# Fused cross-attention and low-bit feed-forward kernel: mask added inside PSUM, exponent read from PSUM, wider column blocks for the attention product, and other places for weight pieces, rows, keys and moves

## The chip, the cores and the metric

One core of one Trainium2 chip. The metric is the device time of one launch in microseconds. TensorE is called PE here (its weight loads PEld), VectorE DVE, ScalarE ACT, GpSimd POOL and SyncE SP.

## What is computed

```python
q = rope((layernorm(x) @ wq) per head)      # 32 query heads of 128
k = rope((ctx @ wk) per head); v = ctx @ wv # 8 key/value heads, each for 4 query heads
scores = q @ k.T / sqrt(128) + mask         # batch 8, 256 rows, 256 keys
x = x + (softmax(scores) @ v) @ wo
w = lut4[o, 4-bit code(qweight)]            # 1024 x 1024
x = x + layernorm(x) @ w.T + bias
```

All is fp32. The norm of every row of the second layer norm is far below the threshold of 64, so the reference's 8-bit branch is never taken and the kernel computes the 4-bit one alone. Each fp32 product is made of three passes over a rounded part (HI) and a rest (LO) of both operands (`PASSES`).

## The kernel before, in words

**Stages.** Batches of keys and values and the decoding of the 4-bit weights come first (to about 394 us), then the attention, then the feed-forward product (from about 2246 us). The change lies in the attention.

**Units, rounds, halves.** The attention runs over `NU` = 256 units. A unit is one query head of one batch entry: 256 rows by 256 keys, scores as two tiles of 128 x 256 in PSUM bank 0 (`s_ps`). Four units in a row (`REP`) share keys and values; 16 units (`UNITS`, 4 batch entries) form a round, which has its own four `wq` and four `wo` pieces; 8 rounds form a half of the batch. Below, "step 4" means a unit whose number leaves 4 when divided by 16.

**PE's order in a step** (L868 to L879): the 6 score matmuls of this unit (`scores`, L800, 256 columns), 12 matmuls of a query projection for a later unit (`query`, L784), in two steps of some rounds four transposes of a normalized row (`turn_side`, L811), 12 matmuls of the output projection of the unit three back (`project`, L862), and in even steps the 6 attention matmuls of the two units before (`attend(u - 2)`, L834, 512 columns: two units at once).

**From scores to transposed probabilities.** DVE adds the mask and takes the row maximum in one instruction per tile (`add_mask`, L1652, result to `probs` in SBUF, the score columns read with a stride of four by `by_blocks`), then negates the maximum (L1659). ACT takes the exponent in place in SBUF (`exponent`, L1177). DVE inverts the sum (`invert`, L1664), POOL scales (`normalize`, L1809), DVE transposes 32 x 32 blocks (`turn_blocks`, L1668), and four DMAs of 64 KB issued by SP spread the blocks over the partitions (`move_blocks`, L590). ACT rounds the result (`turned_high`, L1190), DVE computes the rest (`turned_low`, L1673), and then `attend` may start. ACT's `turned_high` and DVE's `turned_low` of an odd unit stand, in the two engines' orders, behind the exponent and the inversion of the even unit after it. For the units in `PE_TURNS` (1, 253, 254, 255) PE transposes instead (L823) and nothing is moved.

**Weight pieces.** A piece is 512 KB, loaded into the single buffer `raw` (`load_weights`, L395, waits for the rest of the piece before it), rounded by ACT (L1228) and split by DVE (`weights_split`, L1379). `PIECE` puts the pieces of a round at steps 0, 1, 3, 4 (`wo`) and 8, 9, 12, 13 (`wq` of the next round); ACT's and DVE's parts stand at the end of that step. In rounds 1 to 7 one row tile of the next half is layer-normalized on the side: `ROW_AT` (step 0; DVE's `row_var` there, `row_scale` at the end of step 1), `SIDE` (steps 5 and 6, transposed halves split and stored through `raw`).

**SP's order** (L594 to L642) is one queue: values (L461), keys (`load_keys`, L454, waits for the scores of this unit), mask (L448), pieces, moves, rows. Keys for the next four units are loaded at steps that leave 3 when divided by 4, behind the moves of the unit before. The moves of a unit also wait until the attention product two units back has been made (`o_mm`).

**Other DVE work of a step** (L1697 to L1750): `query_cos`, `query_add`, `query_low` (rotary embedding of a projected query, in odd steps), `output_low` (L1678), `add_projection` (four adds of 512 columns, L1694, every fourth step).

**Columns of the attention product.** `pT_keys` gives L834 its 512 moving columns as 16 runs of 32.

```python
pT_keys = R[:, 4608:6656].rearrange("p (l q k j) -> p l k q j", l=2, k=TS, j=QUAD)
def by_blocks(row): return row.rearrange("p (m b) -> p b m", b=P // QUAD)
pe.wait_ge(s_read, u + 1)      # scores(u): the mask of unit u - 1 has read bank 0
```

## Time and profile before

| | us |
|---|---|
| median of 3 runs | 2436.77 (2436.72 to 2442.36) |
| profiled execution | 2438.7 |
| its span | 2436.9 |
| PE busy | 2376.7 (98%) |
| PEld busy | 1999.4 |
| DVE busy | 1658.1 (68%) |
| ACT busy | 1150.0 (47%) |
| POOL busy | 501.6 (21%) |
| mean granted PE clock | 0.997 |

The profiled execution took 2438.7 us, 1.8 us more than its span (what lies around the first and last instruction). Matmuls are pipelined and their ends modelled, so "busy" of PE holds short waits too; the distance from the start of one group of matmuls to the start of the next is the better measure.

### The profile page before, as it was taken

What the parts mean: (1) busy time and instruction counts of PE and PEld (TensorE: products, weight loads), DVE (VectorE), ACT (ScalarE), POOL (GpSimd) and SP (SyncE); (2) the same over time, 40 slices, a digit from 0 to 9 for tenths busy, and PEclk for the clock granted to TensorE, in tenths of its full rate; (3) what the DMA queues carried; (4) which work ended last, traced back from release to release, by engine and by line L of the source; (5) the groups of instructions that cost most, each with busy time, mean ns of one, the idle gap of its engine ahead of it and who ended that gap; (6) DMA issues with size and microseconds to landing.
All of it is one profiled execution on the core that took longest, in us unless ns stands there. A gap on an engine that the chain in (4) does not pass through costs nothing.

```text
span 2436.9 us, 35037 instructions
## 1 busy us (share of the span) xinstructions
PE 2376.7 (98%) x11982; PEld 1999.4 (82%) x11982; DVE 1658.1 (68%) x3810; ACT 1150.0 (47%) x2475; POOL 501.6 (21%) x674
## 2 busy tenths in 40 slices
PE   9999999999999999999999999999999999999999
PEld 8999997878787878787878788778888887887887
DVE  8887776666666666666666666666666666675553
ACT  5555434454645455555544444444444444443110
POOL 1000001222222222222222222222222222222111
PEclk9999999999999999999999999999999999999999
DMA  6466567534343444434357633333333333335211
GB/s 257 159 215 194 183 220 230 158 111 117 108 126 104 113 114 116 114 111 118 106 162 233 196 103 95 99 102 111 96 108 104 96 98 106 103 93 186 87 70 52
DMA packets 323185, 321.44 MB, mean 132 GB/s; under 512 B 31680, under 2 KB 259264, under 8 KB 323008
## 3 DMA queue, kind: packets, MB, share of 16 engines
q1 hardware_dynamic: 323008, 319.20, 43.5%
q8 instruction: 96, 1.57, 0.3%
q14 instruction: 81, 0.66, 0.1%
HBM read 181.73 MB, written 71.30 MB: 104 GB/s over the span
## 4 chain that ended last, share of the span: by engine, by line
PE 75%; DMA 6%; DVE 6%; SPq 4%; ACT 4%; issue 4%; POOL 2%; ACTq 0%; DVEq 0%
PE bank L784 20%; PE bank L862 19%; PE bank L746 7%; PE bank L900 7%; PE bank L723 7%; PE bank L834 7%; PE bank L800 5%; SPq L590 3%; DMA raw<-in_L_xattn_wo 3%; ACT probs L1177 1%; DVE probs L1652 1%; DMA raw<-in_L_xattn_wq 1%; POOL probs L1809 1%; DVE residual L1694 1%; ACT weights_split L1228 1%
## 5 line engine op out<-in xcount | busy, mean ns | idle before, releaser
L784 PE MATMUL bank<-acts_split,weights_split 128*128 128x512 f32 (+1 forms) x3168 | 751.4, 386 | 3.0 <-DVE rope_a L1617 0.4
L862 PE MATMUL bank<-weights_split,small_split 128*128 128x512 f32 x3072 | 741.8, 390 | 4.0 <-DVE small_split L1678 3.7
L862 PEld LDWEIGHTS bank<-weights_split,small_split 128*128 128x128 f32 x3072 | 573.9, 188 | 125.9 <-DVE small_split L1678 7.9
L784 PEld LDWEIGHTS bank<-acts_split,weights_split 128*128 128x128 f32 x3168 | 568.1, 189 | 113.9 <-issue 6.1
L1809 POOL TENSOR_SCALAR probs<-probs,row_numbers 128x256 f32<-128x256 f32 x512 | 289.3, 577 | 1343.6 <-DVE row_numbers L1664 1343.6
L1177 ACT ACTIVATE probs<-probs,row_numbers 128x256 f32<-128x256 f32 x512 | 256.5, 502 | 385.0 <-DVE row_numbers L1659 384.9
L1668 DVE STREAM_TRANSPOSE probs<-probs 128x512 f32<-128x512 f32 x252 | 179.2, 711 | 174.7 <-POOL probs L1809 174.7
L1801 POOL TENSOR_TENSOR rope_x<-rope_x,sin_t 128x512 f32<-128x512 f32 (+1 forms) x132 | 167.1, 1266 | 403.0 <-ACT rope_x L1159 398.0
L834 PE MATMUL bank<-small_split 128*128 128x512 f32 x762 | 208.6, 410 | 41.9 <-DVE small_split L1673 28.7
L800 PEld LDWEIGHTS bank<-small_split 128*128 128x128 f32 x1536 | 219.1, 191 | 33.4 <-DMA small_split<-k_scratch 10.8
L800 PE MATMUL bank<-small_split 128*128 128x256 f32 x1536 | 227.7, 285 | 5.3 <-DMA small_split<-k_scratch 4.6
L1673 DVE TENSOR_TENSOR small_split<-small_split 128x512 fp32r<-128x512 f32 x252 | 179.8, 714 | 61.9 <-ACT small_split L1190 61.9
L834 PEld LDWEIGHTS bank<-small_split 128*128 128x128 f32 x762 | 139.5, 190 | 92.5 <-DVE small_split L1673 38.1
L1652 DVE CUSTOM_DVE_ANT_0 probs<-bank,mask_tile 128x256 f32<-128x256 f32 x512 | 196.6, 421 | 26.3 <-PE bank L800 25.3
L1228 ACT ACTIVATE weights_split<-raw 128x1024 fp32r<-128x1024 f32 x120 | 127.3, 1061 | 161.7 <-DMA raw<-in_L_xattn_wq 81.8
L1379 DVE TENSOR_TENSOR weights_split<-raw,weights_split 128x1024 fp32r<-128x1024 f32 x120 | 146.7, 1223 | 73.2 <-ACT weights_split L1228 72.6
L746 PE MATMUL bank<-small_split,weights_split 128*128 128x256 f32 x1536 | 187.6, 284 | 1.0 <-DVE weights_split L1372 0.6
L746 PEld LDWEIGHTS bank<-small_split,weights_split 128*128 128x128 f32 x1536 | 185.4, 192 | 2.1 <-issue 1.0
L900 PE MATMUL bank<-weights_split,acts_split 128*128 128x512 f32 x768 | 178.5, 391 | 0.0
L723 PE MATMUL bank<-acts_split,small_split 128*128 128x512 f32 x768 | 178.1, 391 | 0.1
L1194 ACT ACTIVATE small_split<-bank 128x512 fp32r<-128x512 f32 x127 | 75.7, 596 | 207.3 <-PE bank L834 207.2
L1664 DVE RECIPROCAL row_numbers<-row_numbers 128x2 f32<-128x2 f32 x256 | 42.4, 166 | 190.4 <-ACT probs L1177 190.4
(120 smaller groups left out, 2284.0 us busy)
## 6 DMA issues: line engine op xcount, KB each, us to landing
small_split<-probs SPq DMA_DIRECT2D x1008, 64.0 KB, 2.1
raw<-in_L_xattn_wq SPq DMA_DIRECT2D x61, 512.0 KB, 3.7
raw<-in_L_xattn_wo SPq DMA_DIRECT2D x60, 512.0 KB, 3.7
k_scratch<-small_split SPq DMA_DIRECT2D x64, 256.0 KB, 2.3
v_scratch<-small_split SPq DMA_DIRECT2D x32, 512.0 KB, 2.9
x_scratch<-raw SPq DMA_DIRECT2D x64, 256.0 KB, 2.8
acts_split<-x_scratch SPq DMA_DIRECT2D x32, 512.0 KB, 5.8
mask_tile<-in_mask_BxSxS_ff SPq DMA_DIRECT2D x64, 256.0 KB, 3.0
```

Of the source, the lines that this page charges most:

```text
L723: done = pe.matmul(wide_ps[t][:, :], ctxT[:, c, a, t * P:(t + 1) * P], wv_s[:, c, m, n * BANK:(n + 1) * BANK], start=c == 0 and k == 0, st ...
L746: done = pe.matmul(k_ps[g % 2], wk_s[:, c, a, g * DK:(g + 1) * DK], ctxT[:, c, m, :], start=c == 0 and i == 0, stop=c == C - 1 and i == 2)
L784: last = pe.matmul(query_bank(j)[:, 0:wide], wq_s[:, h, c, a, :], xT[:, c, m, b * S:b * S + wide], start=c == 0 and i == 0, stop=c == C - ...
L800: last = pe.matmul(s_ps[:, t * S:(t + 1) * S], q_s[:, Q_SLOT[u], a, t * P:(t + 1) * P], k_s[:, m, :], start=i == 0, stop=i == 2)
L834: last = pe.matmul(o_ps[:, :], v_s[:, k, a, :], pT_keys[:, m, k], start=k == 0 and i == 0, stop=k == TS - 1 and i == 2)
L862: last = pe.matmul(out_ps[part][:, :], o_s[:, a, u % 2 * S + t * P:u % 2 * S + (t + 1) * P], wo_s[:, h, m, n * BANK:(n + 1) * BANK], start ...
L900: last = pe.matmul(out_ps[f % 2 * NN + n][:, :], xT[:, c, a, f % HT * P:(f % HT + 1) * P], w4_s[:, c, m, n * BANK:(n + 1) * BANK], start=c ...
L1177: last = act.activation(row, row, ACT.Exp, bias=neg_max[:, u % 2, t:t + 1], accum_out=row_sum[:, u % 2, t:t + 1])
L1652: last = dve.tensor_tensor_reduce(out=by_blocks(probs[:, u % 2, t, :]) if u in PE_TURNS else prob_part(u, t), in0=by_blocks(s_ps[:, t * S: ...
L1668: dve.transpose(prob_rows[:, u % 2, :], prob_rows[:, u % 2, :]).then_inc(p_blocks, 1)
L1673: dve.tensor_tensor(pT_s[:, LO, u % 2, :], source, pT_s[:, HI, u % 2, :].bitcast(F32), ALU.subtract).then_inc(pT_lo, 1)
L1809: done = pool.tensor_scalar(row, row, row_inv[:, u % 2, t:t + 1], 1.0, ALU.mult, ALU.mult)
```

## The change

The score bank is now the place where mask and scores are added (L1652 writes to bank 0, contiguous; the mask is no longer permuted on the host); the exponent reads bank 0 with the stride of four and writes `probs`. So bank 0 is free for the next scores only after the exponent (`exp_done`), and the wait until a `probs` slot has been moved away goes from DVE to ACT. A row of `probs` is laid out so that `pT_keys` has 8 runs of 64 columns. Pieces go to steps 0, 2, 4, 5 and 6, 8, 10, 12; DVE's splits, but for steps 4 and 5, go to the step after, between `invert` and `turn_blocks`. Row tiles go to step 8, their stored halves to steps 13 and 14. In SP's queue most pieces are issued ahead of an odd unit's moves, and of the moves of the unit before a key load two are issued ahead of the keys and two behind, the mask behind them. Units 247 and 251 are turned by PE too. In the first steps some operations of queries and early `wo` pieces trade places.

```diff
-    PE_TURNS = (1, NU - 3, NU - 2, NU - 1)
+    PE_TURNS = (1, NU - 9, NU - 5, NU - 3, NU - 2, NU - 1)
-            PIECE[g * UNITS + (0, 1, 3, 4)[h]] = ("wo", g, h)
+            PIECE[g * UNITS + (0, 2, 4, 5)[h]] = ("wo", g, h)
-            PIECE[g * UNITS + (8, 9, 12, 13)[h]] = ("wq", g + 1, h)
+            PIECE[g * UNITS + (6, 8, 10, 12)[h]] = ("wq", g + 1, h)
+    SAME_STEP = (4, 5)
+    LOAD_LAST = (6, 8)
-    ROW_ROUND = {e: e - A_ROWS + 1 for e in range(A_ROWS, NT)}
-    SIDE = {UNITS * g + 5 + j: (e, j) for e, g in ROW_ROUND.items() for j in range(2)}
-    ROW_AT = {UNITS * g: e for e, g in ROW_ROUND.items()}
+    ROW_AT = {UNITS * (e - A_ROWS) + 8: e for e in range(A_ROWS, NT)}
+    SIDE = {u + 5 + j: (e, j) for u, e in ROW_AT.items() for j in range(2)}
-        pT_keys = R[:, 4608:6656].rearrange("p (l q k j) -> p l k q j", l=2, k=TS, j=QUAD)
+        pT_keys = R[:, 4608:6656].rearrange("p (l a k n) -> p l k a n", l=2, k=TS, n=TS * QUAD)
-        prob_parts = prob_t[:, :].rearrange("p (s b t m) -> p s t b m", s=2, b=P // QUAD, t=TS)
+        prob_parts = prob_t[:, :].rearrange("p (s b k t i) -> p s t b k i", s=2, b=P // QUAD, k=TS, t=TS)
...
-                if u % REP == REP - 1 and u + 1 < NU:
-                    load_keys(u + 1)
-                    load_mask(u + 1)
-                if u % REP == REP - 1 and u in PIECE:
-                    load_weights(u)
+                if u % REP == REP - 1:
+                    if u + 1 < NU:
+                        load_keys(u + 1)
+                    if u - 1 not in PE_TURNS:
+                        move_blocks(u - 1, (2, 3))
+                    if u + 1 < NU:
+                        load_mask(u + 1)
+                if u + 1 in PIECE and (u + 1) % UNITS not in LOAD_LAST:
+                    if u - 1 in SIDE:
+                        sp.wait_ge(x_stored, 4 * 16 * (SIDE[u - 1][0] + 1))
+                    load_weights(u + 1)
...
                 if u % 2 == 0 and u not in PE_TURNS:
-                    move_blocks(u)
-                if u % REP != REP - 2 and u + 1 in PIECE:
+                    move_blocks(u, (0, 1) if u % REP == REP - 2 else range(P // QUAD))
+                if u + 1 in PIECE and (u + 1) % UNITS in LOAD_LAST:
...
-                pe.wait_ge(s_read, u + 1)
+                pe.wait_ge(exp_done, u)
...
             def exponent(u):
+                if u - 2 in PE_TURNS:
+                    act.wait_ge(pT_tr, PE_TURNS.index(u - 2) + 1)
+                elif u >= 2:
+                    act.wait_ge(pT_in[u % 2], 4 * 16 * landed(u - 2))
                 act.wait_ge(s_max, u + 1)
                 for t in range(TS):
-                    row = prob_part(u, t)
-                    last = act.activation(row, row, ACT.Exp,
+                    row, scored = probs[:, u % 2, t, :], s_ps[:, t * S:(t + 1) * S]
+                    if u not in PE_TURNS:
+                        row = prob_parts[:, u % 2, t]
+                        scored = scored.rearrange("p (k i b) -> p b k i", k=TS, i=QUAD)
+                    last = act.activation(row, scored, ACT.Exp,
...
             def add_mask(u):
-                if u - 2 in PE_TURNS:
-                    dve.wait_ge(pT_tr, PE_TURNS.index(u - 2) + 1)
-                elif u >= 2:
-                    dve.wait_ge(pT_in[u % 2], 4 * 16 * landed(u - 2))
                 dve.wait_ge(s_mm, 1 + u + 1)
                 for t in range(TS):
                     last = dve.tensor_tensor_reduce(
-                        out=by_blocks(probs[:, u % 2, t, :]) if u in PE_TURNS else prob_part(u, t),
-                        in0=by_blocks(s_ps[:, t * S:(t + 1) * S]),
-                        in1=mask_t[:, t, :].rearrange("p (b m) -> p b m", b=P // QUAD), scale=1.0, scalar=-3.0e38, op0=ALU.add, op1=ALU.max,
+                        out=s_ps[:, t * S:(t + 1) * S], in0=s_ps[:, t * S:(t + 1) * S],
+                        in1=mask_t[:, t, :], scale=1.0, scalar=-3.0e38, op0=ALU.add, op1=ALU.max,
...
                 invert(u)
                 if u == 0:
                     output_weights_lo(2)
-                if u == 1:
-                    output_weights_lo(3)
+                if u - 1 in PIECE and (u - 1) % UNITS not in SAME_STEP:
+                    split_piece(u - 1)
                 if u % 2 == 0 and u and u - 1 not in PE_TURNS:
                     turned_low(u - 1)
                 if u not in PE_TURNS:
                     turn_blocks(u)
+                if u == 2:
+                    output_weights_lo(3)
...
-                if u in PIECE:
-                    kind, _, h = PIECE[u]
-                    weights_split(A_PIECES + PIECE_AT[u], kind, h)
+                if u in PIECE and u % UNITS in SAME_STEP:
+                    split_piece(u)
```

## Rows read from the trace of the kernel before

**Rows 1.** The page, part 1: busy time and share of the engines.
```profile
PE 2376.7 (98%) x11982; PEld 1999.4 (82%) x11982; DVE 1658.1 (68%) x3810; ACT 1150.0 (47%) x2475; POOL 501.6 (21%) x674
```

**Rows 2.** The chain that ended last: four PE groups (start, time until the next link).
```profile
1029.03 2.75 PE bank L784 x12
1031.78 2.72 PE bank L862 x12
1034.50 0.71 PE bank L800 x6
...
1040.68 1.42 PE bank L834 x6
```

**Rows 3.** Groups of instructions, shapes apart: the attention matmuls, with PE's idle before.
```profile
L834 PE MATMUL bank<-small_split 128*128 128x512 f32 x762 | 208.6, 410 | 41.9 <-DVE small_split L1673 28.7 <-issue 13.1
```

**Rows 4.** Single lines of L800, L834, L862: ns min/median/max, first and last start.
```profile
L800 PE MATMUL bank<-small_split x1536: 274/283/416, 394.2 to 2231.1; 128*128 128x256 f32 x192
...
  DMA small_split<-k_scratch: 15.5, 25
...
L834 PE MATMUL bank<-small_split x762: 397/401/766, 414.2 to 2230.2; 128*128 128x512 f32 x191
...
L862 PE MATMUL bank<-weights_split,small_split x3072: 387/389/504, 422.0 to 2245.6; 128*128 128x512 f32 x192
```

**Rows 5.** Timeline, units 65 to 68 (start, us; in brackets idle before and releaser).
```profile
871.41 0.71 DVE L1668 STREAM_TRANSPOSE probs<-probs 128x512 f32<-128x512 f32 x1 [1.06 <-POOL probs L1809]
...
872.28 0.88 PE L800 MATMUL bank<-small_split 128*128 128x256 f32 x6
...
874.07 1.22 DVE L1379 TENSOR_TENSOR weights_split<-raw,weights_split 128x1024 fp32r<-128x1024 f32 x1
...
876.01 0.42 DVE L1652 CUSTOM_DVE_ANT_0 probs<-bank,mask_tile 128x256 f32<-128x256 f32 x1
...
879.53 1.66 PE L834 MATMUL bank<-small_split 128*128 128x512 f32 x6 [0.91 <-issue]
...
887.22 0.87 PE L800 MATMUL bank<-small_split 128*128 128x256 f32 x6
...
889.75 1.06 ACT L1228 ACTIVATE weights_split<-raw 128x1024 fp32r<-128x1024 f32 x1 [2.36 <-DMA raw<-in_L_xattn_wo]
...
890.85 1.23 DVE L1379 TENSOR_TENSOR weights_split<-raw,weights_split 128x1024 fp32r<-128x1024 f32 x1 [1.34 <-ACT weights_split L1228]
...
891.99 0.42 DVE L1652 CUSTOM_DVE_ANT_0 probs<-bank,mask_tile 128x256 f32<-128x256 f32 x1
...
895.46 1.69 PE L834 MATMUL bank<-small_split 128*128 128x512 f32 x6 [1.57 <-DVE small_split L1673]
```

**Rows 6.** Timeline, units 0 to 2: the first attention product.
```profile
409.24 1.23 DVE L1393 TENSOR_TENSOR weights_split<-residual,weights_split 128x1024 fp32r<-128x1024 f32 x1 [2.89 <-ACT weights_split L919]
...
414.24 2.90 PE L834 MATMUL bank<-small_split 128*128 128x512 f32 x6 [3.39 <-issue]
```

**Rows 7.** One stretch: length, busy us per engine, then granted clock, DMA share, GB/s.
```profile
408.00:426.00 18.00, 14.61 (x58) 11.87 (x58) 10.69 (x24) 8.41 (x19) 4.84 (x6) 0.81 0.21 55
```

**Rows 8.** Groups, shapes apart: operations near to the changed ones on DVE and ACT.
```profile
L1177 ACT ACTIVATE probs<-probs,row_numbers 128x256 f32<-128x256 f32 x512 | 256.5, 502 | 385.0 <-DVE row_numbers L1659 384.9
...
L1652 DVE CUSTOM_DVE_ANT_0 probs<-bank,mask_tile 128x256 f32<-128x256 f32 x512 | 196.6, 421 | 26.3 <-PE bank L800 25.3
...
L1190 ACT ACTIVATE small_split<-small_split 128x512 fp32r<-128x512 f32 x252 | 158.2, 628 | 21.3 <-DMA small_split<-probs 16.0
...
L1194 ACT ACTIVATE small_split<-bank 128x512 fp32r<-128x512 f32 x127 | 75.7, 596 | 207.3 <-PE bank L834 207.2
...
L1270 DVE TENSOR_TENSOR rope_a<-bank,cos_t 128x256 f32<-128x256 f32 x32 | 13.6, 424 | 20.7 <-ACT rope_x L932 20.2
```

**Rows 9.** DMA issues: KB each and median us from issue to landing.
```profile
small_split<-probs SPq DMA_DIRECT2D x1008, 64.0 KB, 2.1
raw<-in_L_xattn_wq SPq DMA_DIRECT2D x61, 512.0 KB, 3.7
```

More of the change, by code:

```diff
@@ L253, in build_xattn_ffn @@
         pT_ps = bank[2]
-        pT_cols = bank[2][:, :].rearrange("p (a t k j) -> p t k a j", t=TS, k=TS, j=QUAD)
+        pT_cols = bank[2][:, :].rearrange("p (a k t j) -> p t k a j", t=TS, k=TS, j=QUAD)
         o_ps = bank[5]
@@ L327, in prob_part @@
         def prob_part(u, t):
-            return probs[:, u % 2, t, :] if u in PE_TURNS else prob_parts[:, u % 2, t]
+            if u in PE_TURNS:
+                return probs[:, u % 2, t, :]
+            return prob_parts[:, u % 2, t].rearrange("p b k i -> p (b k) i")
         def fold(view, units):
@@ L582, in _, with move_blocks @@
             sp.wait_ge(v_stored, 16 + 16 * (NB * len(V_TURNS) - 3))
-            def move_blocks(u):
+            def move_blocks(u, places=range(P // QUAD)):
                 sp.wait_ge(p_blocks, blocks(u))
                 sp.wait_ge(o_mm, 1 + u // 2)
-                for a in range(P // QUAD):
+                for a in places:
                     done = sp.dma_start(pT_moved[:, LO, u % 2, a, :].bitcast(F32),
@@ L844, in attend_one @@
                     for i, (a, m) in enumerate(PASSES):
-                        last = pe.matmul(o_ps[:, half_of], v_s[:, k, a, :], pT_keys[:, m, k, u % 2 * (S // QUAD):(u % 2 + 1) * (S // QUAD)],
+                        last = pe.matmul(o_ps[:, half_of], v_s[:, k, a, :], pT_keys[:, m, k, u % 2 * (P // QUAD):(u % 2 + 1) * (P // QUAD)],
                                          start=k == 0 and i == 0, stop=k == TS - 1 and i == 2)
@@ L1699, in _ @@
                     query_cos(DONE[u - 1])
-                if u >= LAG and u % REP == REP - 1:
+                output_first = u % REP == REP - 1 or u > NU - 14
+                if u >= LAG and u % 2 and output_first:
                     output_low(u - LAG)
@@ L1703, in _ @@
                     add_mask(u)
-                if u >= LAG and u % REP == 1:
+                if u >= LAG and u % 2 and not output_first:
                     output_low(u - LAG)
+                if u == 2:
+                    turned_low(0)
+                if u - 1 in PE_TURNS:
+                    turned_low(u - 1)
                 if u == AHEAD:
@@ L1709, in _ @@
                     query_add(DONE[u - 1])
-                if u - 1 in PE_TURNS:
-                    turned_low(u - 1)
                 if u - 1 in DONE:
@@ L1730, in _ @@
                     query_add(DONE[u])
-                if u % 2 and u - 1 not in PE_TURNS:
+                if u % 2 and u > 1 and u - 1 not in PE_TURNS:
                     turned_low(u - 1)
```

32 lines of the change are left out of this document (15 added, 17 removed).

## The prediction

> **What bounds the kernel now.** The page first: PE is busy 2376.7 of 2436.9 us, DVE 68%, ACT 47% [rows 1]. So PE's order of work sets the time, and only two things can shorten it: cheaper matmuls, or fewer waits between them. The chain of waits gives the undisturbed pace: 0.71 us for the scores, 2.75 for a query projection, 2.72 for an output projection, 1.42 for an attention product [rows 2]. An odd step is the first three, 6.18 us; an even one has the fourth too, 7.60. A round of 16 is 110.2. The scores run from 394.2 to 2231 us [rows 4], 1837 us for 255 steps. Sixteen rounds are 1763; less the last step, narrower or missing queries at the end and missing projections at the start (about 23), plus double queries in the first two steps and the 56 transposes of rows (about 12), that leaves about 1750. So some 87 us are lost in the attention, 5 a round: the most that better order can bring.
>
> Where they are lost, by the groups and single lines: PE sat idle 41.9 us before L834 and at most 15.5 us before the scores for keys [rows 3, 4]. The rest are waits of 0.1 to 0.4 us, which the modelled ends of matmuls cover up, and slow clock after long ones.
>
> Why `attend` waits shows in the timeline [rows 5]. In step 2 (scores at 872.28) it could start 6.18 later, at 878.46, and starts at 879.53: 1.07 late. In step 4 (scores at 887.22) it is due at 893.40 and starts at 895.46: 2.06 late. In both, the mask instruction of that even unit stands 3.5 us ahead of it (876.01 to 879.53, 891.99 to 895.46): mask, exponent, then `turned_high` and `turned_low` of the odd unit, which stand behind them in ACT's and DVE's orders. So the rule for an even step: if its mask starts later than 6.18 - 3.5 = 2.7 us after its scores, PE waits for the difference. Here it was 3.7 and 4.8 us late. What made it late is DVE: in step 1 a piece's split at 874.07 and after it the scale of the row tile, in step 3 a split that waited for ACT, which waited 2.36 us for the piece's DMA. Steps 2 like this one are 8 (about 1.1 us each), steps 4 are 15 (about 1.8 on average, 1.3 to 2.9).
>
> **The change, part by part.** All against the profiled execution's 2438.7 us, which is 1.9 above the median of 2436.77; the saving is carried over to the median.
>
> *Splits into DVE's gap.* In an odd step DVE idles 1.06 us for POOL between `invert` and `turn_blocks` (the first line of [rows 5]). A split is 1.22. Six of eight splits go there, so each costs 0.16 us of DVE's order instead of 1.22, and a split after step 3's mask no longer waits for a DMA issued in the same step. With that, step 4's mask should start at 4.8 - 1.22 - 1.3 (the wait) + 0.16, about 2.4 us: no wait of PE, barely. Of 15 x 1.8 = 27 us I take 24, keeping a fifth of a us a round for moves that land late. In step 2 the row's scale leaves too: 3.7 - 1.06 - 0.72 = 1.9 us. I take 8 of 8 x 1.1 = 9 us.
>
> *Rows to steps 8, 13 and 14.* The scale (0.72 us from the end of the split, 875.29, to the mask [rows 5]) now burdens step 10, in seven rounds, which loses its split of step 9 in exchange. Nothing; at worst 7 x 0.5 = 3.5.
>
> *Splits of steps 4 and 5 stay at the step's end.* Step 6's mask gets 1.22 us in front; by the pattern of steps 10 and 14 before, which had the same split in front and hardly waited, it comes to about 2.6, just under 2.7. I take 3 us lost; 0 to 15 x 1 = 15 are the ends.
>
> *Start.* `attend(0)` came 3.39 us late, behind a split that waited 2.89 for ACT [rows 6], and the clock granted over the 18 us around it was 0.81 [rows 7], which is 0.19 x 18 = 3.4 us more at the lower of the two levels. The early `wo` piece 3 moves behind it. I take 5 of 6.8.
>
> *Keys.* They are issued behind two moves instead of four, and no longer behind a late `turn_blocks`, so about 1.2 us earlier. The 15.5 us counts PEld's waits; the ones seen were up to 1 us. I take 8; 4 to 12.
>
> *Wider runs.* L834 takes 1.42 / 6 = 237 ns a matmul, L862 with the same 512 columns in one run 2.72 / 12 = 227 [rows 2]; their shortest rows differ by the same 10 ns [rows 4]. If it is the 16 runs, 8 runs give back half: 762 x 5 ns = 4 us. Ends: 0 (it is something else) and 7.6.
>
> *Mask in PSUM, exponent from PSUM.* The mask instruction writes to PSUM, which no DVE row shows; it reads the bank with a stride of four now at 421 ns, and a DVE instruction of the same size that reads a bank contiguously takes 424 [rows 8]. I take 421 after; ends 380 and 480. ACT reads PSUM faster than SBUF, 596 against 628 ns for 512 columns [rows 8], so the exponent (502) could lose 30 ns; but with a stride of four, which no ACT row shows. I take 480 and 1100 (below) as ends, 490 as value, by DVE's row. Worth nothing on PE: the exponents' gain of 0.02 us a unit ends in slack.
>
> *The new wait.* Scores of unit u wait for the exponent of u - 1 instead of its mask. What is queued behind is all of PE. The mask of unit 66 starts 3.7 us after its scores [rows 5]; from there two masks and two exponents take 2 x 421 + 2 x 502 ns [rows 8], with the small ones between some 2.1 us: 5.8, where the next scores come after 7.6 at the earliest. In an odd step a mask even 2.4 us late gives 4.5 of 6.18. Slack 1.7, so nothing; an exponent pair 1.7 us longer would hold PE up in odd steps. The wait for moved `probs`, now on ACT, is for moves issued a step earlier: they land 2.1 us after issue [rows 9], over 3 us ahead.
>
> *Two more units turned by PE.* Eight transposes of 128 columns, under 0.5 us a unit, for eight DMAs fewer and two steps near the end without their landing. Nothing; -3 to +1.
>
> *SP.* A piece's issue before an odd unit's moves is one more issue of 0.6 us, but DVE's split, for which it waits, ends as `turn_blocks` (0.71 us) begins, so it is out before the moves may go. Nothing; the landing is a rival.
>
> *Small waits after splits in the gap* (query_cos 0.16 later, PE's next query waits for it in some steps): 3 us lost.
>
> Sum: 24 + 8 + 5 + 8 + 4 - 3 - 3 = 43 us. 2438.7 - 43 = 2395.7 for a profiled execution, **2394** for the median.
>
> **A rule that speaks against it.** DVE's row says that a stride of four in PSUM costs nothing. The Trainium skill (Advanced Engine Details and Errata, PSUM Cachelines) says that PSUM has lines of 8 bytes and that every two consecutive elements should be contiguous for best throughput; the trace disagrees for DVE and has nothing for ACT. By the skill the exponent would be slower; by the row not.
>
> **The rivals.**
>
> *The exponent is slow with the stride (slower, 8%).* L1190 takes 628 ns for 512 columns, at most 1.23 ns each; a read at half pace adds up to 0.31 us to an exponent, at a quarter 0.93, twice per unit. At 0.62 us a unit the 2.7 us of the rule become 2.1: step 6 waits 0.5, steps 4 and 8 (2.4) 0.3, and the queries behind `query_cos` about 0.5 in four steps: 3 us x 16 = 48, time 2442. At 1.86 a unit all eight even steps wait, 0.9 on average above the half-pace case: 2500 or more. It decides from an exponent of about 800 ns. For it: only the missing row. Against: DVE's.
>
> *Moves behind pieces land late (18%).* Five odd units a round (steps 15, 1, 3, 9, 11) now send their moves right behind 512 KB that take 3.7 us, where a move takes 2.1 [rows 9]. Up to 1.6 later. The worst placed moves (turned 0.3 after the next scores, four issues, landing near 4.3) have 0.4 us of slack against 6.18 - 1.5. At 0.8 later PE loses 0.4 x 5 x 16 = 32: 2426; at 1.6, 96: 2490. Against: the fourth move leaves 2.4 us after the piece, and most units will be turned earlier. 14% for 2412 to 2435, 4% for above.
>
> *The wait moves to step 6 (14%).* Piece 5 is loaded only when piece 4 is split; if it lands late, DVE waits as step 3 did, and 15 x 1.9 = 28 us come back: 2422.
>
> *Nothing happens* (the waits have another cause): within the chance of no change.
>
> **How the numbers follow.** 60% for the forecast, own range 2378 (all ends good) to 2412. Over 0.3%, 7 us, is what a measurement tells: faster below 2429.5, slower above 2444. Faster: 60 + 14 + 9 = 83%; same 7% ; slower 10% (most of the exponent's 8, and 3 of late moves). The range 2378 to 2430 leaves out some 6% below and 15% above.
>
> **What would show it.** L834 idle from 41.9 to under 12 us; L834 groups 1.39 to 1.40 instead of 1.42; mask of step 4 starting about 2.4 us after the scores, of step 2 about 1.9; L1177 at 480 to 500 ns; L800 idle for keys near nothing; DVE's wait for POOL down from 1.06 to nothing in steps with a split; the clock never at 0.81 near 414 us. Wrong: L1177 above 700; L1190 waiting for DMA over 30 us in all (16.0 now, rows 8); L834 waits gathered in step 6.

## The result, and the profile after

| | before | after |
|---|---|---|
| median, us | 2438.90 (4 runs) | 2419.68 (4 runs, 2417.57 to 2420.95) |
| ratio, 95% interval | | 0.9919, 0.9902 to 0.9936 |
| profiled execution, us | 2438.7 | 2419.55 |
| its span, us | 2436.9 | 2417.8 |
| mean granted PE clock | 0.997 | 0.999 |

The change is faster by 19 us (the medians' difference; the before's median here has one run more than the one shown above). 43 were forecast. From the first scores to the last, the attention took 1836.3 us before and 1815.3 after: 21 us, so the whole difference lies there (the rest of the program took 2 us longer).

The page after, part 1 (busy time) and the groups of part 5 (busy, mean ns of one | PE's or the engine's idle before it, and what ended it):

```profile
PE 2360.4 (98%) x11990; PEld 2001.1 (83%) x11990; DVE 1665.4 (69%) x3808; ACT 1132.6 (47%) x2475; POOL 573.7 (24%) x674
...
L791 PE MATMUL bank<-acts_split,weights_split 128*128 128x512 f32 (+1 forms) x3168 | 753.2, 387 | 40.5 <-DVE rope_a L1633 40.4
...
L1824 POOL TENSOR_SCALAR probs<-probs,row_numbers 128x256 f32<-128x256 f32 x512 | 365.5, 726 | 1276.0 <-DVE row_numbers L1675 1276.0
L1193 ACT ACTIVATE probs<-bank,row_numbers 128x256 f32<-128x256 f32 x512 | 238.2, 470 | 373.8 <-DVE row_numbers L1670 373.7
L1664 DVE CUSTOM_DVE_ANT_0 bank<-bank,mask_tile 128x256 f32<-128x256 f32 x512 | 206.6, 445 | 109.3 <-PE bank L807 109.3
...
L807 PE MATMUL bank<-small_split 128*128 128x256 f32 x1536 | 224.0, 282 | 1.7 <-ACT probs L1193 1.7
L841 PE MATMUL bank<-small_split 128*128 128x512 f32 x762 | 196.3, 393 | 4.6 <-issue 2.7
...
L1206 ACT ACTIVATE small_split<-small_split 128x512 fp32r<-128x512 f32 x250 | 158.1, 632 | 35.4 <-DMA small_split<-probs 26.0
```

Beside [rows 1, 3, 8]: `attend` (now L841) waits 4.6 us where it waited 41.9. That is the wait that the change was forecast to remove, and it is gone. But the query projection (now L791) waits 40.5 us, for `query_cos` on DVE (L1633). And POOL is busy 573.7 us instead of 501.6 [rows 1], with the same 674 instructions: its scaling of a row tile (now L1824) takes 726 ns. The two groups in the kernel before:

```profile
L784 PE MATMUL bank<-acts_split,weights_split 128*128 128x512 f32 (+1 forms) x3168 | 751.4, 386 | 3.0 <-DVE rope_a L1617 0.4
...
L1809 POOL TENSOR_SCALAR probs<-probs,row_numbers 128x256 f32<-128x256 f32 x512 | 289.3, 577 | 1343.6 <-DVE row_numbers L1664 1343.6
```

3.0 us of waiting and 577 ns. In the changed kernel, the waits of PE grouped by waiter and releaser, over the attention (us in all, times, longest):

```profile
PE bank L791 <- DVE rope_a L1633: 40.4, 55, 1.8
PE bank L869 <- DVE small_split L1689: 3.4, 7, 0.9
PE bank L841 <- issue: 2.7, 5, 1.4
```

How the new wait comes about, in the timeline of an odd step, unit 71 (start, duration, engine, line; in brackets idle before and releaser):

```profile
915.97 0.17 DVE L1675 RECIPROCAL row_numbers<-row_numbers 128x2 f32<-128x2 f32 x1 [1.15 <-ACT probs L1193]
...
916.05 1.20 DVE L1395 TENSOR_TENSOR weights_split<-raw,weights_split 128x1024 fp32r<-128x1024 f32 x1
...
916.23 1.83 POOL L1824 TENSOR_SCALAR probs<-probs,row_numbers 128x256 f32<-128x256 f32 x2 [6.10 <-DVE row_numbers L1675]
...
918.09 0.71 DVE L1679 STREAM_TRANSPOSE probs<-probs 128x512 f32<-128x512 f32 x1 [0.83 <-POOL probs L1824]
...
918.73 0.65 DVE L1633 SCALAR_TENSOR_TENSOR rope_a<-bank,cos_t 128x512 f32<-128x512 f32 x1
...
919.44 3.02 PE L791 MATMUL bank<-acts_split,weights_split 128*128 128x512 f32 x12 [1.00 <-DVE rope_a L1633]
```

The split (L1395) stands where DVE used to wait for POOL. POOL's pair of row tiles, started beside it, takes 1.83 us; in the kernel before it took, in two steps after each other (odd, then even):

```profile
870.45 0.93 POOL L1809 TENSOR_SCALAR probs<-probs,row_numbers 128x256 f32<-128x256 f32 x2 [6.24 <-DVE row_numbers L1664]
...
878.41 1.36 POOL L1809 TENSOR_SCALAR probs<-probs,row_numbers 128x256 f32<-128x256 f32 x2 [5.66 <-DVE row_numbers L1664]
```

0.93 us with DVE idle, 1.36 with `turned_low` beside it. These are no chance picks: in the changed kernel's trace the pair takes 1.82 to 1.83 us beside each of 90 splits, and in the kernel before 0.93 in the 136 cases without a longer DVE instruction beside it and 1.36 (median) in the 116 with `turned_low`. In the changed kernel `turn_blocks` (L1679) thus still waits 0.83 us for POOL, as DVE waited 1.06 before [rows 5]: the split filled DVE's gap, and the gap was made longer by it. `query_cos` behind it comes late, and PE waits 1.00 us. The theory from here on: **a split in the gap slows the very POOL instruction that the gap waits for.** The rivals: the forecast's 0.16 us for each split is right and PE waits for something that comes later in DVE's order; or DVE is merely busy for too long.

### The profile page after: what moved, and what is told of

Its sections match the earlier page's. It is cut to its first block, busy times and chain, and to the rows that moved or that the text cites. A ratio compares the mean times of both kernels' runs of the same rounds, so it can differ in the third digit from the quotient of the medians.

```text
span 2417.8 us, 35170 instructions
## 1 busy us (share of the span) xinstructions
PE 2360.4 (98%) x11990; PEld 2001.1 (83%) x11990; DVE 1665.4 (69%) x3808; ACT 1132.6 (47%) x2475; POOL 573.7 (24%) x674
## 4 chain that ended last, share of the span: by engine, by line
PE 55%; DVE 20%; POOL 9%; ACT 7%; issue 4%; DMA 3%; SPq 2%; ACTq 0%; DVEq 0%
PE bank L791 14%; PE bank L869 12%; POOL probs L1824 8%; PE bank L907 7%; PE bank L753 7%; PE bank L730 6%; ACT probs L1193 5%; DVE residual L1705 5%; PE bank L841 4%; DVE bank L1664 3%; PE bank L807 3%; DVE probs L1679 2%; DMA small_split<-probs 2%; DVE rope_a L1633 2%; SPq L593 1%
## 5 line engine op out<-in xcount | busy, mean ns | idle before, releaser
L791 PE MATMUL bank<-acts_split,weights_split 128*128 128x512 f32 (+1 forms) x3168 | 753.2, 387 | 40.5 <-DVE rope_a L1633 40.4
L869 PE MATMUL bank<-weights_split,small_split 128*128 128x512 f32 x3072 | 741.3, 390 | 3.5 <-DVE small_split L1689 3.4
L791 PEld LDWEIGHTS bank<-acts_split,weights_split 128*128 128x128 f32 x3168 | 567.3, 189 | 155.2 <-DVE rope_a L1633 29.0
L869 PEld LDWEIGHTS bank<-weights_split,small_split 128*128 128x128 f32 x3072 | 574.4, 188 | 124.1 <-DVE small_split L1689 5.3
L1824 POOL TENSOR_SCALAR probs<-probs,row_numbers 128x256 f32<-128x256 f32 x512 | 365.5, 726 | 1276.0 <-DVE row_numbers L1675 1276.0
L1193 ACT ACTIVATE probs<-bank,row_numbers 128x256 f32<-128x256 f32 x512 | 238.2, 470 | 373.8 <-DVE row_numbers L1670 373.7
L1664 DVE CUSTOM_DVE_ANT_0 bank<-bank,mask_tile 128x256 f32<-128x256 f32 x512 | 206.6, 445 | 109.3 <-PE bank L807 109.3
L1679 DVE STREAM_TRANSPOSE probs<-probs 128x512 f32<-128x512 f32 x250 | 177.7, 711 | 145.1 <-POOL probs L1824 145.1
L841 PE MATMUL bank<-small_split 128*128 128x512 f32 x762 | 196.3, 393 | 4.6 <-issue 2.7
L1172 ACT ACTIVATE small_split<-rope_a 128x512 fp32r<-128x512 f32 (+1 forms) x132 | 81.7, 619 | 213.7 <-DVE rope_a L1640 212.8
L841 PEld LDWEIGHTS bank<-small_split 128*128 128x128 f32 x762 | 140.5, 188 | 41.5 <-issue 9.6
L1206 ACT ACTIVATE small_split<-small_split 128x512 fp32r<-128x512 f32 x250 | 158.1, 632 | 35.4 <-DMA small_split<-probs 26.0
```

The lines of the kernel that those rows point to most:

```text
L791: last = pe.matmul(query_bank(j)[:, 0:wide], wq_s[:, h, c, a, :], xT[:, c, m, b * S:b * S + wide], start=c == 0 and i == 0, stop=c == C - ...
L841: last = pe.matmul(o_ps[:, :], v_s[:, k, a, :], pT_keys[:, m, k], start=k == 0 and i == 0, stop=k == TS - 1 and i == 2)
L869: last = pe.matmul(out_ps[part][:, :], o_s[:, a, u % 2 * S + t * P:u % 2 * S + (t + 1) * P], wo_s[:, h, m, n * BANK:(n + 1) * BANK], start ...
L1193: last = act.activation(row, scored, ACT.Exp, bias=neg_max[:, u % 2, t:t + 1], accum_out=row_sum[:, u % 2, t:t + 1])
L1664: last = dve.tensor_tensor_reduce(out=s_ps[:, t * S:(t + 1) * S], in0=s_ps[:, t * S:(t + 1) * S], in1=mask_t[:, t, :], scale=1.0, scalar=- ...
L1679: dve.transpose(prob_rows[:, u % 2, :], prob_rows[:, u % 2, :]).then_inc(p_blocks, 1)
```

## The experiments

### Is the split in the gap the cost?

Two kernels, each the changed one with one block edited. The first leaves the six gap splits of a round out:

```diff
                 if u - 1 in PIECE and (u - 1) % UNITS not in SAME_STEP:
-                    split_piece(u - 1)
+                    split_piece(u - 1, True)
```

(With `True` it waits for ACT as before and then does one operation on two columns.)

> The changed kernel, but DVE's six splits a round that stand between the inversion and the block transpose are replaced by an instruction on 2 columns (the LO part of those weight pieces is not computed). Theory 1 (POOL's scaling and DVE's split disturb each other: in the changed kernel's trace the pair of scalings takes 1.83 us beside a split and 0.93 alone, so a split in the gap costs the transpose 0.9 us and not 0.16, and makes query_cos and with it PE's next query late): POOL's L1824 falls from 726 ns to 600 or less, PE's idle before the queries from 40 us to under 12, time 2420 to 2385-2400. Theory 2 (the query waits come from the mask written to PSUM, 445 ns and a longer read of its maximum, and from the scores' wait for the exponent): idle before the queries stays over 25 us, time over 2410.

The second keeps them and moves them ahead of `invert`, to the time in which DVE waits for the exponent and POOL has nothing to do:

```diff
+                if u - 1 in PIECE and (u - 1) % UNITS not in SAME_STEP:
+                    split_piece(u - 1)
                 invert(u)
                 if u == 0:
                     output_weights_lo(2)
-                if u - 1 in PIECE and (u - 1) % UNITS not in SAME_STEP:
-                    split_piece(u - 1)
```

> The changed kernel, with the six splits a round moved ahead of the inversion, into the time in which DVE waits for the exponent and POOL is idle. Theory 1: POOL's scaling back under 620 ns; DVE's idle of 0.57 to 1.15 us there is filled, so the transpose comes 0.1 to 0.7 us later than without a split, not 0.9; idle before the queries 10 to 20 us; time 2395 to 2408, a gain of 12 to 25 us over the changed kernel. Theory 2: the split's own 1.22 us is what makes query_cos late wherever it stands before it: time within 5 us of 2420.

Measured: 2378.01 us (ratio to the kernel before 0.9743, 0.9729 to 0.9758) with the splits left out, 2378.33 (0.9745, 0.9731 to 0.9760) with them moved. The second does all of the work and takes no longer than the first, which leaves some out. The place of the split is thus worth 41 us (2419.68 - 2378.33). Both went further than had been expected (2385 to 2400, and 2395 to 2408); that moving a split would give back as much as leaving it out was not foreseen. The page of the moved one:

```profile
L791 PE MATMUL bank<-acts_split,weights_split 128*128 128x512 f32 (+1 forms) x3168 | 749.4, 386 | 6.7 <-DVE rope_a L1633 5.0
...
L1824 POOL TENSOR_SCALAR probs<-probs,row_numbers 128x256 f32<-128x256 f32 x512 | 279.7, 559 | 1302.8 <-DVE row_numbers L1675 1302.8
```

The wait before the queries is down from 40.5 to 6.7 us and POOL's instruction from 726 to 559 ns, below the 577 of before (562 with the splits left out). The same places in its timeline, an odd step:

```profile
901.47 1.22 DVE L1395 TENSOR_TENSOR weights_split<-raw,weights_split 128x1024 fp32r<-128x1024 f32 x1
...
902.71 0.17 DVE L1675 RECIPROCAL row_numbers<-row_numbers 128x2 f32<-128x2 f32 x1
...
902.97 0.93 POOL L1824 TENSOR_SCALAR probs<-probs,row_numbers 128x256 f32<-128x256 f32 x2 [6.10 <-DVE row_numbers L1675]
903.94 0.71 DVE L1679 STREAM_TRANSPOSE probs<-probs 128x512 f32<-128x512 f32 x1 [1.06 <-POOL probs L1824]
...
904.57 0.65 DVE L1633 SCALAR_TENSOR_TENSOR rope_a<-bank,cos_t 128x512 f32<-128x512 f32 x1
905.28 3.01 PE L791 MATMUL bank<-acts_split,weights_split 128*128 128x512 f32 x12
```

From `invert` to `turn_blocks` it is 1.23 us here and 2.12 us in the changed kernel: 0.89 us later behind a split. PE's idle before the queries fell by 34 of these 41 us; the rest shows as no wait in the profile. That settles where the time goes, not by which mechanism.

### Is it that DVE is busy, or what it touches?

In both kernels the splits of four of the gaps (steps 3, 7, 9, 11, the first in unit 7 and the last in unit 235: 59 gaps) give way to two DVE operations of 256 columns; the other gap splits are left out as above. In one the operations read and write PSUM alone (a bank that is free there, times zero), in the other they are the first half of the split itself: each reads two operands in SBUF and writes to SBUF.

```diff
+                    if 2 < at < NU - UNITS and at % UNITS in (2, 6, 8, 10):
+                        dve.tensor_scalar(pT_ps[:, 0:S], pT_ps[:, 0:S], 0.0, None, ALU.mult)
+                        dve.tensor_scalar(pT_ps[:, S:2 * S], pT_ps[:, S:2 * S], 0.0, None, ALU.mult).then_inc(w_lo, 1)
```

> The changed kernel with the splits in the gap left out as in gap_splits_left_out, but in steps 3, 7, 9 and 11 (from unit 3 to unit 239) DVE does two instructions of 256 columns there, PSUM bank 2 to itself, about 0.8 us, beside POOL's two scalings (the LO parts of the six pieces a round are not computed). Theory 1 (POOL and DVE share a way into SBUF: what slows POOL is DVE's SBUF traffic, not DVE's being busy): POOL's L1828 mean stays at 555 to 575 ns (562 without any gap instruction), time 2376 to 2381. Theory 2 (any DVE instruction beside POOL slows it, or a busy DVE alone makes the transpose late): POOL's mean at 590 or more, time 2385 or more.

```diff
+                    if 2 < at < NU - UNITS and at % UNITS in (2, 6, 8, 10):
...
+                        for low, whole, high in pieces:
+                            last = dve.tensor_tensor(low, whole, high.bitcast(F32), ALU.subtract)
+                        last.then_inc(w_lo, 1)
```

> The counterpart of gap_op_in_psum: in the same steps DVE does two instructions of 256 columns in the gap, about as long, but with all operands in SBUF (the first halves of the split). Theory 1: POOL's pair takes about 0.5 us longer in these steps, as beside turned_low, so L1828's mean rises to 600 to 640 ns, and the time to 2383 to 2395. Theory 2 (place does not matter): same POOL mean and time as gap_op_in_psum.

Measured: 2379.47 us (0.9764, 0.9749 to 0.9778) with PSUM, 2388.37 (0.9804, 0.9790 to 0.9819) with SBUF, in one set with the changed kernel at 2418.20. The timelines at one gap, PSUM first:

```profile
903.50 0.41 DVE L1658 TENSOR_SCALAR bank<-bank 128x256 f32<-128x256 f32 x1
...
903.68 0.94 POOL L1832 TENSOR_SCALAR probs<-probs,row_numbers 128x256 f32<-128x256 f32 x2 [6.10 <-DVE row_numbers L1683]
...
903.83 0.42 DVE L1659 TENSOR_SCALAR bank<-bank 128x256 f32<-128x256 f32 x1
```

and the same gap with SBUF:

```profile
906.27 0.74 DVE L1664 TENSOR_TENSOR weights_split<-raw,weights_split 128x256 fp32r<-128x256 f32 x2
...
906.45 1.29 POOL L1838 TENSOR_SCALAR probs<-probs,row_numbers 128x256 f32<-128x256 f32 x2 [6.10 <-DVE row_numbers L1689]
```

DVE is busy for about as long in both (0.41 + 0.42 against 0.74 us). POOL's pair takes 0.94 us beside the one and 1.29 beside the other. So it is not that DVE is busy, but what its operations touch. The means of POOL's instruction (563 and 606 ns) and both times are as expected for this theory. PE's idle before the queries is 5.0 us in the first and

```profile
L791 PE MATMUL bank<-acts_split,weights_split 128*128 128x512 f32 (+1 forms) x3168 | 749.6, 386 | 16.8 <-DVE rope_a L1633 16.6
```

in the second. The rival "DVE is merely busy" falls.

The two kernels differ in more than the place, though: the PSUM operations have one input, those in SBUF two. The changed kernel's own trace tells the two apart. Near its end DVE adds a projection, with one input in SBUF, one in PSUM and the result in SBUF, beside POOL's pair:

```profile
2209.78 2.46 DVE L1705 TENSOR_TENSOR residual<-residual,bank 128x512 f32<-128x512 f32 x4
...
2209.96 0.94 POOL L1824 TENSOR_SCALAR probs<-probs,row_numbers 128x256 f32<-128x256 f32 x2 [3.53 <-DVE row_numbers L1675]
```

The pair takes 0.94 us, as if alone. So DVE's working in SBUF isn't enough; the slow pairs have a DVE instruction with two inputs in SBUF beside them.

The Trainium skill (SBUF — State Buffer, the section on the two separate sides) says that DVE and GpSimd share a pair of ports, and that of a DVE operation with two SBUF inputs and a GpSimd operation that reads SBUF, whichever starts first holds the pair for its whole instruction while the other is blocked. The trace agrees for a DVE that starts first, by the time in which both ran: the split ended 1.02 us after POOL's pair began (916.05 + 1.20 - 916.23), and the pair took 0.90 more; the halves ended 0.56 after it (906.27 + 0.74 - 906.45), and it took 0.36 more. POOL stood still for most of what they shared. Where POOL was first, as with `turned_low`, DVE lost time too: L1673 before takes 0.68 us away from POOL, and in the even steps 0.76 (0.93 at most).

### The parts of the change by themselves

The orders alone (pieces, rows, keys, moves, the start; mask and exponents as before, runs of 32), as edits of the kernel before:

```diff
-            PIECE[g * UNITS + (0, 1, 3, 4)[h]] = ("wo", g, h)
+            PIECE[g * UNITS + (0, 2, 4, 5)[h]] = ("wo", g, h)
-            PIECE[g * UNITS + (8, 9, 12, 13)[h]] = ("wq", g + 1, h)
+            PIECE[g * UNITS + (6, 8, 10, 12)[h]] = ("wq", g + 1, h)
...
+                if u - 1 in PIECE and (u - 1) % UNITS not in SAME_STEP:
+                    split_piece(u - 1)
```

> The kernel before with only the orders changed (pieces, rows, SP's queue, splits in the gap, two more units turned by PE); mask to SBUF, exponent in SBUF, 16 runs of 32. Theory 1: L834's idle gone as in the changed kernel, idle before the queries about 30 to 45 us, matmuls of the attention product at 237 ns: 2424 to 2432. Theory 2 (the query waits belong to the PSUM part): idle before the queries under 15 us, time 2395 to 2412.

and the rest alone (on the kernel before, in its order):

```diff
-                pe.wait_ge(s_read, u + 1)
+                pe.wait_ge(exp_done, u)
...
-                        out=by_blocks(probs[:, u % 2, t, :]) if u in PE_TURNS else prob_part(u, t),
-                        in0=by_blocks(s_ps[:, t * S:(t + 1) * S]),
...
+                        out=s_ps[:, t * S:(t + 1) * S], in0=s_ps[:, t * S:(t + 1) * S],
...
-        pT_keys = R[:, 4608:6656].rearrange("p (l q k j) -> p l k q j", l=2, k=TS, j=QUAD)
+        pT_keys = R[:, 4608:6656].rearrange("p (l a k n) -> p l k a n", l=2, k=TS, n=TS * QUAD)
```

> The kernel before with only the mask added in PSUM, the exponent from PSUM, the scores' wait for the exponent and the 64-column runs; all orders, pieces, rows and moves as before. Theory 1 (the attention product's 237 ns become 227, 7.6 us; the rest of this part is worth little; the orders gave the rest): time 2428 to 2434 against 2438.9. Theory 2 (this part costs time through the slower mask): 2436 to 2450.

Measured: 2413.11 (0.9888, 0.9871 to 0.9905) and 2445.55 (1.0016, 1.0006 to 1.0026). The orders bring the whole gain and by the medians, of two sets, 6.6 us more than the changed kernel has; the rest takes time away from it. With 2413.11 the orders alone came out between the two ranges expected. They have the same new wait, somewhat smaller than the 30 to 45 us expected, which rules out that it belongs to the PSUM part alone:

```profile
L789 PE MATMUL bank<-acts_split,weights_split 128*128 128x512 f32 (+1 forms) x3168 | 751.7, 386 | 29.5 <-DVE rope_a L1622 28.9
```

Then the two parts of the rest, one each. Runs of 64 columns alone, where mask and exponent stay in SBUF:

```diff
-                return row.rearrange("p (m b) -> p b m", b=P // QUAD)
+                return row.rearrange("p (k i b) -> p b k i", k=TS, i=QUAD)
...
-                        out=by_blocks(probs[:, u % 2, t, :]) if u in PE_TURNS else prob_part(u, t),
+                        out=by_blocks(probs[:, u % 2, t, :]) if u in PE_TURNS else prob_parts[:, u % 2, t],
```

> The kernel before with the 64-column runs alone, mask and exponent in SBUF. Theory 1 (runs of 32 cost 10 ns a matmul and runs of 64 nothing, 762 x 10 ns): L834's median 401 ns becomes 389, time 7.6 us less, 2430 to 2434 for 2440.3. Theory 2 (DVE pays for the finer blocks in its mask instruction, over 450 ns): 2436 or more.

Mask and exponent in PSUM alone, with runs of 32:

```diff
-                pe.wait_ge(s_read, u + 1)
+                pe.wait_ge(exp_done, u)
...
-                        out=by_blocks(probs[:, u % 2, t, :]) if u in PE_TURNS else prob_part(u, t),
-                        in0=by_blocks(s_ps[:, t * S:(t + 1) * S]),
...
+                        out=s_ps[:, t * S:(t + 1) * S], in0=s_ps[:, t * S:(t + 1) * S],
```

> The kernel before with mask and exponent in PSUM alone, runs of 32 as before. Theory 1 (this part costs 11 to 14 us by the two pairs): 2449 to 2456 against 2440.3. Theory 2 (the runs give less than 7.6, and this part costs little): 2442 to 2447.

Measured: 2439.63 (0.9988, 0.9975 to 1.0001) for the runs, 2449.38 (1.0024, 1.0008 to 1.0041) for PSUM. The runs first. A single attention matmul, in the line's own statistics (ns min/median/max) with both parts on the kernel before and in the changed kernel:

```profile
L836 PE MATMUL bank<-small_split x762: 387/389/796, 415.2 to 2232.2; 128*128 128x512 f32 x191
```

```profile
L841 PE MATMUL bank<-small_split x762: 387/389/504, 412.0 to 2210.5; 128*128 128x512 f32 x191
```

against 397/401 before [rows 4] and, with the orders alone,

```profile
L839 PE MATMUL bank<-small_split x762: 397/400/506, 411.9 to 2204.8; 128*128 128x512 f32 x191
```

With runs of 64 it takes what L869 takes for one run of 512: all of the 10 ns come back, not half. Yet on the kernel before they bring 3 us of the 7.6, and the interval reaches to nothing; 2430 to 2434 had been expected. The groups of that kernel show where the rest stays:

```profile
L836 PE MATMUL bank<-small_split 128*128 128x512 f32 x762 | 202.8, 402 | 46.7 <-DVE small_split L1675 33.8
...
L1654 DVE CUSTOM_DVE_ANT_0 probs<-bank,mask_tile 128x256 f32<-128x256 f32 x512 | 196.6, 421 | 23.6 <-PE bank L802 22.8
```

6 us less busy, 4.8 us more idle than in [rows 3], and the mask instruction is as quick as before (421 ns), so DVE doesn't pay for the finer blocks. `attend` waits for its input in step 4 of every round and in step 2 of about half of them, and a quicker PE only comes to that wait sooner.

PSUM then: the price can be read in two more rows, the accumulator read that follows each mask instruction, after (first) and with mask and exponent in SBUF (second; the kernel below):

```profile
L1664 DVE DVE_READ_ACCUMULATOR2_ANT row_numbers<- 128x1 f32 x512 | 71.8, 140 | 0.0
```

```profile
L1664 DVE DVE_READ_ACCUMULATOR2_ANT row_numbers<- 128x1 f32 x512 | 43.0, 84 | 0.0
```

The mask instruction itself goes from 421 to 445 ns and its accumulator read from 84 to 140; the exponent from 502 to 470. These durations overlap, so they don't add up to what DVE's order loses. From the start of a unit's first mask instruction it is 0.80 us to the negation before and 0.90 after, and 2.13 and 2.22 us to the inversion (medians): 0.10 us more on DVE, 0.08 more for the chain, the quicker exponent included. On the kernel before, where a late mask makes PE wait in steps 2 and 4, the PSUM part costs 2449.38 - 2442.86 = 6.5 us (2 to 10 by the interval), where 11 to 14 had been expected. In its trace `attend` waits 43.7 us instead of 41.9, and the queries wait 4.4 us for `query_cos` instead of 0.4; the scores never wait for the exponent.

### The version without the faults

The moved splits together with mask and exponent in SBUF and runs of 64, the better half of each pair:

```diff
-                pe.wait_ge(exp_done, u)
+                pe.wait_ge(s_read, u + 1)
...
+                        out=by_blocks(probs[:, u % 2, t, :]) if u in PE_TURNS else prob_parts[:, u % 2, t],
+                        in0=by_blocks(s_ps[:, t * S:(t + 1) * S]),
...
+                if u - 1 in PIECE and (u - 1) % UNITS not in SAME_STEP:
+                    split_piece(u - 1)
                 invert(u)
...
```

> The orders of split_before_invert (2378.3) with the mask written to SBUF and the exponent in SBUF as before, but with the 64-column runs (DVE writes and reads in blocks of 4 x 2 x 32). Theory 1 (mask and exponent in PSUM cost time: the two parts together were worth +4 us on the kernel before and +6.6 on its changed orders, though the runs give back 7.6 of PE, so PSUM itself costs 11 to 14): 2364 to 2372. Theory 2 (PSUM's share only lengthens a chain that now has slack): 2374 to 2382.

Measured: 2374.06 us (0.9716, 0.9697 to 0.9734), the fastest of all. It was run again, in one set with the changed kernel:

> The fastest version once more, beside the changed kernel on one chip: 2374.1 in its first runs. Expected 2371 to 2377, 43 to 48 us below the changed kernel. If PSUM's share of 4 us was the difference of two chips only, it lands at 2377 or above.

> The changed kernel as it is, beside the others on one chip: 2419.7 in its first runs; both theories expect 2416 to 2423.

2372.39 us (0.9738, 0.9724 to 0.9753) and 2418.20 (0.9927, 0.9910 to 0.9944): 46 us apart. 41 of them are the place of the splits. The other 4 to 5 would be the place of the mask (2378.33 - 2374.06), but those two times are from two sets and the intervals of their ratios overlap, so this small share isn't shown on the changed orders; it is on the kernel before. It is in any case far from the 11 to 14 us of the first theory. The groups of the fastest kernel, beside those of [rows 8] and of after:

```profile
L1184 ACT ACTIVATE probs<-probs,row_numbers 128x256 f32<-128x256 f32 x512 | 256.6, 502 | 333.3 <-DVE row_numbers L1671 333.2
L1664 DVE CUSTOM_DVE_ANT_0 probs<-bank,mask_tile 128x256 f32<-128x256 f32 x512 | 197.1, 423 | 125.2 <-PE bank L807 122.8
```

### The order around the key loads

To the kernel with moved splits, SP's old order is given back around the keys: all four moves, then the keys, then the mask.

```diff
-                if u % REP == REP - 1:
-                    if u + 1 < NU:
-                        load_keys(u + 1)
-                    if u - 1 not in PE_TURNS:
-                        move_blocks(u - 1, (2, 3))
-                    if u + 1 < NU:
-                        load_mask(u + 1)
+                if u % REP == REP - 1 and u + 1 < NU:
+                    load_keys(u + 1)
+                    load_mask(u + 1)
...
-                    move_blocks(u, (0, 1) if u % REP == REP - 2 else range(P // QUAD))
+                    move_blocks(u)
```

> split_before_invert with SP's queue around a key load as before: all four moves, then keys, mask, piece. Theory 1 (the split of the moves lets keys land before the scores of every fourth step): PE's idle before the scores for keys comes back, 4 to 12 us: 2382 to 2390. Theory 2 (with nothing else late the keys were in time anyway): 2376 to 2380.

Measured: 2381.13 (0.9750, 0.9731 to 0.9768), 2.8 us above the 2378.33 of the same kernel with the new order, measured in another set, and just between the two ranges expected. The ratios' difference, 0.0005, is smaller than their intervals, so the runs don't separate the two times. The rows show that the mechanism is there: PE waits for keys again, which it does nowhere in the changed kernel:

```profile
L803 PE MATMUL bank<-small_split 128*128 128x256 f32 x1536 | 225.7, 283 | 5.6 <-DMA small_split<-k_scratch 3.7
```

## Why the forecast was right in direction and wrong in size

*What bounds the kernel, and the waits of `attend`* (terms of 24 and 8 us): right. The mask of step 4 starts 2.33 us after its scores (median; forecast 2.4) and that of step 2 1.62 (forecast 1.9), below the limit of 2.7. Only step 8's is above it, at 3.11, and `attend` hardly waits there, since PE has already waited about 1.1 us before that step's query. In the later rounds of the moved-split kernel a round takes 110.3 us, the undisturbed pace of 110.2 that the forecast had worked out. (In the trace of the kernel before, `attend` waited 24.0 us in 15 rounds' step 4 and 11.0 us in nine steps 2; only seven rounds have a row tile, where the forecast counted eight.) The idle before `attend` fell by 37 us, and the moved-split kernel shows what comes of it when nothing takes its place: 62 us off the kernel before (2440.29 - 2378.33), where the terms without the last one summed to 46. Of the other 16 us, 1 to 3 can be named by the clock. In its profiled run the kernel before was at the lower level twice more, 3.4 us each time (from 1246.4 and 1321.5 us), which costs 3.4 us in all, and the moved-split kernel never in the attention; over all runs of that set the mean clocks, 0.9976 and 0.9993, differ by 4 us, the start's 3.4 included. The wider runs give up to 3.6 more, and the loss of 3 us taken for step 6 didn't come. The rest was not taken apart; `attend`'s idle alone was 5 us more than the two terms, which the smaller gain of the keys, below, takes back.

*Splits into DVE's gap* ("each costs 0.16 us of DVE's order instead of 1.22", and "small waits after splits in the gap ... 3 us lost"): this is **the step that failed**. It took the gap as idle time of fixed length and let a split of 1.22 us fill its 1.06. But the gap was the time of another engine's SBUF instruction, and the split made that instruction 0.90 us longer. Its cost to the order is about 0.9 us each, not 0.16, and where the next query waits for `query_cos`, in steps 4, 8, 10 and 12, PE stood still: 41 us by the time of the kernel with moved splits, where 3 were taken. What was there to be read: the pair of 1.36 us beside `turned_low` against 0.93 alone. The mean of 577 ns mixes the two, and only the timeline tells them apart; `turned_low` took 0.76 us there, so the loss of 0.43 would have warned that a split of 1.22 costs some 0.7 (an estimate, 0.43 / 0.76 x 1.22).

*Start* (5 us): it happened, and was lost again at once. The stretch of [rows 7] after:

```profile
408.00:426.00 18.00, 15.37 (x75) 12.18 (x74) 11.77 (x30) 8.94 (x20) 5.10 (x8) 1.00 0.25 69
```

The granted clock is 1.00 there instead of 0.81 and `attend(0)` doesn't wait. But the first round as a whole took 118.7 us, where it took 116.0. Further on, at step 8:

```profile
444.78 1.06 ACT L1244 ACTIVATE weights_split<-raw 128x1024 fp32r<-128x1024 f32 x1 [4.11 <-DMA raw<-in_L_xattn_wq]
...
453.68 4.61 PE L791 MATMUL bank<-acts_split,weights_split 128*128 128x512 f32 x12 [1.81 <-DVE rope_a L1633]
```

a piece lands late, PE waits 1.81 us, and the 12 matmuls behind it take 4.61 us where 12 take 3.02 in the step above: the granted clock was at half from 454.7 to 458.1 us. But the clock isn't what gave the gain back. In the second trace of the changed kernel it never fell, the same matmuls take 3.03 us,

```profile
453.74 3.03 PE L791 MATMUL bank<-acts_split,weights_split 128*128 128x512 f32 x12 [1.80 <-DVE rope_a L1633]
```

and the round still takes 118.9. What both traces share is 5 us of waits before four queries of this round, which the kernel before doesn't have. With moved splits they are 2.4 us and the round takes 116.6, so the failed step accounts for some 2 us; why even this round isn't shorter than the 116.0 of before stays open.

*Keys* (8 us): the direction right by the rows, the size off. 3 us by the medians of the pair above and 1 by its ratios, not clear of noise; PE's own waits for keys came to 4.6 us before. The 15.5 us of [rows 4] counted weight loads that run ahead of their matmuls, and most of that PE didn't feel.

*Wider runs* (4; ends 0 and 7.6): per matmul the upper end was right, all 10 ns. On the kernel before 3 us of the 7.6 came back, for want of anything to feed PE sooner.

*Mask and exponent in PSUM*: taken as nothing on PE, by 421 and 490 ns. The exponent took 470, below even the lower end of 480 (the upper end of 1100 was a slip: at half pace, by the rival's own numbers, one exponent would take 800); the mask took 445, inside its ends; the accumulator read, 84 ns before and 140 after, was in no row that the forecast had looked at. Together they add 0.10 us a unit to DVE's order, as above. Of the rule on PSUM's lines of 8 bytes (the Trainium skill, Advanced Engine Details and Errata, PSUM Cachelines): the trace disagrees, for ACT too. An exponent that reads PSUM with a stride of four takes 470 ns, less than 502 from SBUF, and as long as the exponents of the units turned by PE, which read the bank without a stride (459 to 476). *The rival of the slow exponent* needed 800 and fell; the wait of scores for the exponent is 1.7 us in all, one event.

*Step 6* (3 us, and the rival at 14%): its mask starts 2.57 us after the scores (median), and PE waits 0.4 us before its `attend` over all rounds.

*Late moves* (18%): ACT waits 26.0 us for moves instead of 16.0, under the 30 set as a mark, and the 4.6 us that PE waited before `attend` are the most that it can have cost there.

So the likeliest case ran as written but for one term, and what stood at -3 was -41. The waits of `attend`, the keys, runs and clock were worth some 60 us together, more than forecast; two thirds of it went into a new wait that the change itself made. That 2419.68 lies inside the forecast's range, 2378 to 2430, and close to the 2422 of the rival of step 6, is luck: neither the range nor that rival had this wait in it.

## What to carry to other kernels

An idle stretch of an engine that waits for another is free only if the work put there doesn't slow the one waited for: here DVE's gap beside a GpSimd instruction was no place for an operation with two inputs in SBUF, while the time in which DVE waits for ScalarE was. Before filling such a gap, look for the same instruction of the other engine beside different neighbours (0.93 and 1.36 us here) instead of its mean. And a group that waits for its input gains nothing from being made cheaper until the wait is gone.

## What the runs showed of the hardware

POOL's scaling of two tiles of 128 x 256 in SBUF took 0.93 us alone, 0.94 beside DVE operations in PSUM, 0.94 beside a DVE addition with one input in PSUM and one in SBUF, 1.29 beside 0.74 us of DVE's subtraction in SBUF, and 1.83 beside 1.20 us of it; DVE's split, which started first, was not slowed (1.20 and 1.22 us); `turned_low`, which started behind POOL, was (0.76 and 0.68). A matmul of 512 fp32 columns took the same 387 to 389 ns in 8 runs of 64 columns as in one run, and 10 ns more in 16 runs of 32. DVE's add-and-maximum over 256 columns took 24 ns more with its result in PSUM instead of SBUF, and the accumulator read behind it 56 ns more, two thirds above the 84 before. ACT's exponent took 470 ns reading PSUM with a stride of four and 459 to 476 without one.
